# Value products of four key tiles in one block, and the order of the other products around them, in a gated cross-attention block with a mixture of experts

## The reference, cut to what matters

```
x: (32, 56, 128)   ctx: (32, 1500, 128)   16 heads of depth 8   160 experts, 8 chosen
q = layernorm(x) @ Wq.T + bq;  k = ctx @ Wk.T + bk;  v = ctx @ Wv.T + bv
scores = q.k / sqrt(8);  attn = softmax(scores);  out = (attn.v) @ Wo.T + bo
x = x + tanh(g_xattn) * out
logits = layernorm(x) @ router_w.T + expert_bias;  top 8 of sigmoid(logits), normalised, * 2.5
x = x + tanh(g_ffn) * (sum over experts of weight * silu(x @ w_gate.T) @ w_down.T + shared expert)
```

## Time and profile before

| what | value |
|---|---|
| median of 3 runs | 1172.58 us (1171.59 to 1176.96) |
| the profiled execution's own time | 1173.53 us |
| its span in the profile | 1172.0 us |
| instructions | 37843 |
| PE, DVE, ACT, POOL busy over the span | 91%, 83%, 72%, 51% |
| mean granted PE clock | 0.981 of full speed |

### The profile page before, as it was taken

One profiled execution on the slowest core, in us unless ns is written; L12 is line 12 of the kernel. 1 busy time (PEld: TensorE's weight loads), 2 busy tenths in 40 slices (PEclk: granted clock), 3 DMA queues, 4 the chain that ended last, 5 costly groups with the idle time before them and its releaser, 6 DMA issues.

```text
span 1172.0 us, 37843 instructions
## 1 busy us (share of the span) xinstructions
PE 1071.9 (91%) x12090; PEld 709.5 (61%) x12090; DVE 978.0 (83%) x1680; ACT 849.1 (72%) x1790; POOL 596.8 (51%) x1011
## 2 busy tenths in 40 slices
PE   1566989999999999999999999778999999999998
PEld 0244767777777777777777676544555555555554
DVE  2774878888888888888888789658999999999998
ACT  1334767776777777677777677557888888888887
POOL 7788588888889888888888871000000000000000
PEclk9988999999999999999999999889999999999999
DMA  8869778969889797897989852134767676767773
GB/s 130 144 118 182 156 131 177 163 151 160 157 174 166 154 163 149 169 171 151 159 158 174 150 118 61 19 124 131 235 231 234 223 240 221 238 228 232 231 226 125
DMA packets 200998, 197.04 MB, mean 168 GB/s; under 512 B 161183, under 2 KB 167391, under 8 KB 200966
## 3 DMA queue, kind: packets, MB, share of 16 engines
q1 hardware_dynamic: 189446, 175.64, 67.3%
q0 software_dynamic: 11520, 20.99, 6.4%
HBM read 109.96 MB, written 12.55 MB: 105 GB/s over the span
## 4 chain that ended last, share of the span: by engine, by line
PE 48%; issue 13%; POOL 13%; DVE 10%; SPq 10%; DMA 2%; ACT 1%; POOLq 1%; DVEq 0%; ACTq 0%
PE bank L1256 15%; PE bank L1228 15%; PE bank L1067 5%; PE bank L1081 5%; DVE part_max L835 5%; SPq L334 4%; PE bank L1098 4%; SPq L378 3%; DVE rec L936 2%; POOL q_st L574 2%; POOL ctx_parts L497 2%; PE bank L1134 2%; POOL w_in L458 2%; POOL w_in L460 2%; POOL q_blk L551 1%
## 5 line engine op out<-in xcount | busy, mean ns | idle before, releaser
L640 ACT ACTIVATE p_exp<-bank 125x448 f32<-125x448 f32 x768 | 400.4, 544 | 207.1 <-PE bank L1081 206.2
L835 DVE TENSOR_REDUCE part_max<-bank 128x1 f32<-128x500 f32 x672 | 419.8, 670 | 82.7 <-PE bank L1098 82.2
L1081 PE MATMUL bank<-q_st,k_stk 97*125 97x224 f16 x1536 | 277.3, 265 | 19.6 <-DMA q_st<-neg_row 9.9
L1098 PE MATMUL bank<-kparts,q_blk 128*128 128x500 f16 x672 | 256.8, 383 | 20.9 <-DVE part_max L835 17.4
L1081 PEld LDWEIGHTS bank<-q_st,k_stk 97*125 97x125 f16 x1536 | 198.4, 139 | 85.7 <-ACT p_exp L640 18.8
L1256 PE MATMUL bank<-ctT,w_ring 128*128 128x448 f16 x960 | 234.0, 353 | 3.0 <-DVE ctT L978 3.0
L729 ACT ACTIVATE ctT<-bank 128x448 f32<-128x448 f32 x320 | 174.0, 544 | 40.0 <-PE bank L1228 15.8
L978 DVE TENSOR_TENSOR ctT<-k_stk,ctT 128x448 f16<-128x448 f32 x320 | 197.6, 618 | 0.3 <-ACT ctT L735 0.2
L1067 PE MATMUL bank<-p_exp,v_sb 125*25 125x168 f32 (+1 forms) x6144 | 190.0, 265 | 0.6 <-ACT p_exp L640 0.6
L735 ACT ACTIVATE ctT<-k_stk 128x448 f16<-128x448 f32 x320 | 181.9, 568 | 3.5 <-DVE k_stk L972 3.4
L1228 PE MATMUL bank<-q_hi,w_ring 128*128 128x448 f16 x640 | 173.9, 354 | 2.4 <-ACT k_stk L717 2.4
(11 more groups left out here) (139 smaller groups left out, 1234.0 us busy)
## 6 DMA issues: line engine op xcount, KB each, us to landing
v_sb<-c_scratch SPq DMA_DIRECT2D x114, 448.0 KB, 4.0
k_stk<-kparts SPq DMA_DIRECT2D x384, 93.8 KB, 5.1
ctx_in<-in_ctx_dram SPq DMA_DIRECT2D x31, 750.0 KB
k_stk<-c_scratch SPq DMA_DIRECT2D x38, 448.0 KB, 3.9
w_scratch<-w_out POOLq DMA_DIRECT2D x80, 128.0 KB, 6.6
w_in<-in_L_ffn_w_gate_dram POOLq DMA_DIRECT2D x160, 32.0 KB, 3.9
w_in<-in_L_ffn_w_down_dram POOLq DMA_DIRECT2D x80, 64.0 KB, 7.0
v_sb<-c_scratch SPq DMA_DIRECT2D x6, 336.0 KB, 4.8
```

What stands on the lines that cost most here:

```text
L640: act.activation(p_exp[0:KP, j % PR, f * 448:(f + 1) * 448], ST[f][0:KP, 0:448], ACT.Exp).then_inc(exp_done, 1)
L835: v.reduce_max(part_max[:, i // NCH, i % NCH:i % NCH + 1], SM[i % NSM][:, 0:CK], axis=AX.X).then_inc(sm_maxed, 1)
L1081: last = pe.matmul(ST[f][0:KP, (g % 2) * GC:(g % 2 + 1) * GC], k_stk[0:97, u, g, j * KP:(j + 1) * KP], q_st[0:97, u, g, :, :].rearrange("p ...
L1098: pe.matmul(SM[i % NSM][:, 0:CK], rows, kparts[:, u, 0, c * CK:(c + 1) * CK], start=True, stop=True).then_inc(sm_done, 1)
```

## The change

- The ring `p_exp` gets six tiles instead of four; the raw weights, which are used at the start alone, lie in it instead of in a tensor of their own.
- AV products come in blocks of four key tiles, in slots 3, 7 and 11, instead of blocks of two, in slots 1, 3, 5, 7, 9 and 11.
- Key products move from slots 2, 6, 10 to 1, 5, 9; V products from 0, 4, 8 to 2, 6, 10.
- The spread and `normalise` move from slot 6 to 4, the spread ahead of the slot's second maximum; the output product moves from slot 11 to 8. The second V product of a step now waits for `normalise`, the third for the update of x.
- Maxima: `MAXIMA` gives their number in each slot, one in slots 5, 6 and 11, two in all others. The last one is now in slot 11, where PE also transposes the maximum.
- DVE's list follows: the copy and `normalise` stand ahead of the slot's second maximum; what empties the key bank comes after it.

```diff
-    PR = 4
+    PR = 6
+    AVB = 4
-    SPREAD_AT, OUT_AT, NEG_AT = 6, KT - 1, KT - 1
+    K_AT, V_AT = 1, 2
+    SPREAD_AT, OUT_AT, NEG_AT = 4, 8, KT - 1
+    MAXIMA = (2, 2, 2, 2, 2, 1, 1, 2, 2, 2, 2, 1)
...
-        w_raw = sb("w_raw", [128, 4, D])
...
-        q_tmp = e_words[:, NP * D:NP * D + TC]
+        q_tmp = e_words[:, (NP + 4) * D:(NP + 4) * D + TC]
+        w_raw = e_words[:, NP * D:(NP + 4) * D].rearrange("p (n c) -> p n c", c=D)
...
         def chunks_at(k, place):
-            i = 2 * k + place
-            return [i] if i < MT * NCH else []
+            return [sum(MAXIMA[:k]) + place] if place < MAXIMA[k] else []
...
# ACT
-                        if f == 0 and k % TPC == 1 and on(step, 1):
+                        if f == 0 and k % TPC == V_AT + 1 and on(step, 1):
                             values(back(step, 1), k // TPC)
...
-                    if k % TPC == 2:
+                    if k % TPC == K_AT:
                         act.wait_ge(kp_done, b * NCH + (c + 1))
...
# DVE
                     for i in chunks_at(k, 0) if on(step, 1) else []:
                         maxima(step, i)
-                    for i in chunks_at(k, 1) if on(step, 1) else []:
-                        maxima(step, i)
-                    evacuate(step, k - 1)
                     if on(step, 3) and k == LAG:
...
                     if on(step, 3) and k == SPREAD_AT:
                         normalise(step)
-                    if on(step, 1) and k == NEG_AT - 1:
+                    for i in chunks_at(k, 1) if on(step, 1) else []:
+                        maxima(step, i)
+                    evacuate(step, k - 1)
+                    if on(step, 1) and k == NEG_AT:
...
-                evacuate(step, KT - 1)
...
-                    if k % TPC == 2:
+                    if k % TPC == K_AT:
                         dve.wait_ge(k_hi_done, b * NCH + (c + 1))
...
# PE
-                    if values_there and jv % 2:
-                        value_product(bv_, jv - 1)
-                        value_product(bv_, jv)
+                    if values_there and jv % AVB == AVB - 1:
+                        for j in range(jv - AVB + 1, jv + 1):
+                            value_product(bv_, j)
+                    if on(step, 3) and k == SPREAD_AT:
...
+                            pe.wait_ge(v_copied, num(back(step, 1)) * NCH + 1)
...
+                        pe.wait_ge(o_copied, b + 1)
+                        pe.matmul(VB[:, 0:OC], den_spread[:, :], o_raw[:, :], start=True, stop=True).then_inc(spread_done, 1)
                     for i in chunks_at(k, 1) if on(step, 1) else []:
                         maxima(step, i)
...
-                    if on(step, 0) and k % TPC == 2:
+                    if on(step, 0) and k % TPC == K_AT:
...
-                    if on(step, 1) and k % TPC == 0:
+                    if on(step, 1) and k % TPC == V_AT:
                         until(pe, v_copied, b * NCH + c)
-                        if on(step, 4) and c == 0 and back(step, 4)[1] == 1:
-                            pe.wait_ge(x2_done, back(step, 4)[0] + 1)
-                        if on(step, 3) and c == 2:
+                        if on(step, 3) and c == 1:
                             pe.wait_ge(nrm_done, num(back(step, 3)) + 1)
+                        if on(step, 3) and c == 2 and back(step, 3)[1] == 1:
+                            pe.wait_ge(x2_done, back(step, 3)[0] + 1)
...
                     if on(step, 3) and k == OUT_AT and back(step, 3)[1] == 1:
...
-                            pe.wait_ge(v_copied, num(back(step, 1)) * NCH + NCH)
+                            pe.wait_ge(v_copied, num(back(step, 1)) * NCH + 2)
```

More of the change, by code:

```diff
@@ L1109, in body @@
                             maxima(step, i)
-                    if values_there and jv % 2:
-                        value_product(bv_, jv - 1)
-                        value_product(bv_, jv)
+                    if values_there and jv % AVB == AVB - 1:
+                        for j in range(jv - AVB + 1, jv + 1):
+                            value_product(bv_, j)
+                    if on(step, 3) and k == SPREAD_AT:
+                        b = num(back(step, 3))
+                        if on(step, 1):
+                            pe.wait_ge(v_copied, num(back(step, 1)) * NCH + 1)
+                        else:
+                            pe.wait_ge(v_copied, B * NCH)
+                            pe.wait_ge(x2_done, b // 2)
+                        pe.wait_ge(o_copied, b + 1)
+                        pe.matmul(VB[:, 0:OC], den_spread[:, :], o_raw[:, :], start=True, stop=True).then_inc(spread_done, 1)
                     for i in chunks_at(k, 1) if on(step, 1) else []:
@@ L1136, in body @@
                         last.then_inc(vp_done, 1)
-                    if on(step, 3) and k == SPREAD_AT:
-                        b = num(back(step, 3))
-                        if on(step, 1):
-                            pe.wait_ge(v_copied, num(back(step, 1)) * NCH + 2)
-                        else:
-                            pe.wait_ge(v_copied, B * NCH)
-                            pe.wait_ge(x2_done, b // 2)
-                        pe.wait_ge(o_copied, b + 1)
-                        pe.matmul(VB[:, 0:OC], den_spread[:, :], o_raw[:, :], start=True, stop=True).then_inc(spread_done, 1)
                     if on(step, 1) and k == NEG_AT:
```

## The result

| what | before | after |
|---|---|---|
| median of six runs each, on the same chip | 1173.40 us (1171.59 to 1176.96) | 1182.57 us (1179.32 to 1182.98) |
| the profiled execution's own time | 1173.53 us | 1179.32 us |
| its span | 1172.0 us | 1177.8 us |
| mean granted PE clock | 0.981 | 0.972 |

The ratio is 1.0082, 95% interval [1.0066, 1.0099]: slower by 9 us, and 1.6 us above the upper end of the range. The changed kernel once more on another chip gave 1178.05 us (1173.39 to 1182.00, six runs) against 1171.69, ratio 1.0049 [1.0033, 1.0066]. So the change costs 6 to 9 us, and the second median, 1178.05 us, lies inside the range.

The account below looks back on a forecast made before the run. PE and POOL were both taken as full with the same period, POOL's list deciding. The loop stayed unchanged and the tail gave -0.5: 1173.0 us profiled, median 1.0 lower, 1172.0 us; range 1167 to 1181.

Parts of the forecast that it names:

- POOL's list is untouched, a faster PE would wait for the row, and a slower one has room: Loop up to POOL's last one: no change, with POOL at 21.0 us a step against 20.7 of PE.
- AV blocks, -0.6 a step: PE's AV products: a block of four takes 1.68 us against 1.80, with fewer switches, saving 0.6 us a step.
- New waits, 1.4 us in place of 0.7: PE's list in the new order: waits in short slots, after key copies and for `normalise`, adding 0.7 us a step.
- DVE about 1 us idle before the copy, below the step: DVE's list: stands about 1 us until the block of four ends; 19 to 20 us a step, below the step.
- The ring of six, the output product, the transfers: nothing: `p_exp` with six tiles, output product moved to slot 8, SP's transfers: each claimed to cost or gain no time.
- Tail, -0.5: Last steps after POOL's last loop: a block of two no longer stands between scores in the very last, 0.5 us less.
- PE was the bound: Rival for the loop: POOL only looks full, its hidden waits shrink with PE; 17 us less, 1155 us; chance 0.10.
- V product of slot 6: Rival in PE's list: it waits for `normalise` 0.7 us instead of 0.4; each 0.5 beyond costs 14 us, 1186; chance 0.17.
- Switches not saved: Rival in the AV blocks: tiles wait for exponentials, PE's step is 21.3 us, total 1180 us; chance 0.03.
- The rule weighed: Skill page's rule for the most-contended engine: POOL leads at 87% against 74% weight loads of PE; no change in the sum.

Follow-up runs that it names:

- b_after: Changed kernel with the reciprocal written back into its own PSUM bank, so DVE's product has one SBUF operand: 1174.83 us, ratio 1.0025.
- bp_after: Changed kernel with POOL's store and loads of an expert preparation moved behind the next split, and the reciprocal in its PSUM bank: 1167.25 us, ratio 0.9959.
- the one edit tried: Changed kernel with AV blocks of two again in the last two steps alone: 1178.38 us, ratio 1.0064.
- bp_before: Kernel before with POOL's store and loads of an expert preparation moved behind the next split, and the reciprocal in its PSUM bank: 1161.22 us, ratio 0.9912.
- lighter list: Kernel before with POOL's store and loads of an expert preparation moved behind the next split or `q_st`: 1166.14 us, ratio 0.9949.
- the shorter wait: Changed kernel where the V product in slot 6 waits for the reciprocal instead of the product behind it: 1176.82 us, ratio 1.0042.

## Why the prediction was wrong, point by point

**The step that failed** is the one in the sum that reads "POOL's list is untouched, a faster PE would wait for the row, and a slower one has room". The list is untouched in its instructions, not in its time. POOL's two steps went from 41.31 to 41.69 us, because the change moved DVE's `o_nrm` from places where POOL computed nothing onto two of its casts. `b_after` shows it: with the product's second operand in its bank POOL is back at 41.36. With the collision POOL and PE are equally long again, the room for PE's longer order is gone, and what POOL loses in stoppages comes on top. The 24 steps can be parted into twelve steady pairs and the stoppages:

| us | steady pairs | stoppages | 24 steps |
|---|---|---|---|
| before | 12 x 41.34 = 496.1 | 5.9 | 502.0 |
| after | 12 x 41.66 = 499.9 | 5.1 | 505.0 |
| after, again | 499.9 | 4.4 | 504.3 |
| b_after | 12 x 41.68 = 500.2 | 2.4 | 502.6 |

With the collision taken away, what PE's longer period costs comes back through fewer stoppages all but 0.6 us: the room that the prediction counted on is there, and the loop costs close to the nothing that it forecast, instead of 2.3 to 3.0.

This step is not the whole miss. For the profiled execution I had 1173.0 us, and it took 1179.3. Of these 6.3 us the loop is 3.0, the tail 2.7 (2.2 more instead of 0.5 less), the start 0.6. In the second profile, 8.5 us above the one before, the loop is 2.3, the start 1.7, the three steps behind the loop 3.0 and the tail 1.5. And `b_after` is still 3 us slower than the kernel before (1.0025). Why the first six executions have a median 3.2 us above the profiled one no trace shows; with 1178.05 us, the other median, the range would have held.

**AV blocks, -0.6 a step.** Nearly right. A block of 64 matmuls takes 1.66 us to the next maximum (427.23 to 428.89 in the changed kernel), predicted 1.68; the scores ahead of it took 0.28 to 0.34, mostly 0.33, where I had 0.28, which takes about 0.1 us off the saving (an estimate from these rows).

**New waits, 1.4 us in place of 0.7.** Places right, sum nearly. The V product waits 0.35 (I had 0.4). PE's own steps are 20.53 and 21.15, predicted 20.4 and about 21.0: 41.68 for two instead of 41.4. `bp_after` gives the same 41.68 with POOL out of the way, so it is PE's order with DVE's and ACT's answers, and 0.28 us of it was missing from my walk. In 24 steps that is 3.4 us, nearly all that the order costs there; I had left it out of the sum because POOL's average of 42.3 would hide it.

**DVE about 1 us idle before the copy, below the step.** The idle time is right (1.15). That DVE does not matter is wrong. Its busy share says so and its place does not: a product of 0.57 instead of 0.39 makes PE's step longer by the same 0.18, in both orders, as long as PE waits for it.

**The ring of six, the output product, the transfers: nothing.** The ring alone changes nothing within 0.1%. The output product and the transfers were not tried alone.

**Tail, -0.5.** Wrong in sign: 1.5 and 2.2 us more in the two executions of the changed kernel, 0.5 and 1.4 more in the two with the bank. I read no granted clock there. PE is at half clock for 10.2 to 13.6 us there instead of 6.8, and blocks of four take 3.2 us in it instead of 1.7 (PE's timeline, after):

```profile
761.22 3.20 PE L1068 MATMUL bank<-p_exp,v_sb 125*25 125x168 f32 x64
```

That this makes the difference is argued from these rows; the one edit tried changed the clock as well as the blocks. The three steps before the last transpose scatter by 3 us from one execution to the next (69.4 and 72.3 for the same kernel), and remain open.

**The rivals.** *PE was the bound* (0.10): no. PE does have 41.35 of its own, as `bp_before` shows with POOL waiting for it, so its period was no image of POOL's, but with a shorter list for PE the new order is not shorter either. *V product of slot 6* (0.17): the sign is right and the wait has the size I gave it, 0.35 for 0.4. Its condition did not come true: PE's step, 20.83 on average, stayed under POOL's 21.0. The wait has a share all the same, 0.07 to 0.09 of the 0.16 us by which PE's step grew, and it is the way by which a longer product reaches PE. Without it the changed kernel still has 1.0042. *Switches not saved* (0.03): they are saved. That two full engines both get longer at once, by different causes, was in no case. Such a case, "both lists longer by 0.3 to 0.4 a pair", gives 12 x 0.35 = 4 us in the loop, 1176 us, and 1178 to 1179 with the tail as measured: nearer, and still short of 1182.57.

**The rule weighed** named POOL as the engine to relieve first. The lighter list alone gained 5.5 us, at the start, and nothing in the 24 steps; only with the collision removed did the loop give 5.8 us (502.0 to 496.2). Relieving the leader was right and not enough.

## What to carry to other kernels

When two engines are full with the same period, moving work of a third engine can lengthen either of them: look at what runs beside what, not only at who waits for whom. Before calling a list untouched, check that its instructions keep their neighbours on the other engines; here a product that read two operands from SBUF, moved by 2 us, cost POOL 0.36 us a pair of steps, and reading one of them from the bank took that away at no cost to the product. Take an edit as refuted only where no other list stands in its way: the shorter wait brought next to nothing beside a full POOL, and 14 us once POOL was free. An edit of the tail wants the granted clock read first: in these profiles PE's clock fell around pauses of 1.73 to 4.42 us, though not around each, and the edit meant for that stretch made the stretch longer.

A version that beats both kernels came out twice: 1161.22 us (the old order, lighter list, reciprocal in the bank) and 1161.37 us (the new order, lighter list, shorter wait), ratios 0.9912 [0.9887, 0.9936] and 0.9911 [0.9887, 0.9934].

## What the runs showed of the hardware that I had not expected

**DVE and POOL hold each other up when DVE's product has two operands in SBUF.** With one of them in PSUM it takes 0.390 to 0.393 us in all 96 cases of four kernels; with both in SBUF it takes 0.39 where POOL stands still. Beside POOL's work one of the two is longer, or both: mostly 0.56 to 0.68 for the product with the lighter list, or a product of 0.39 and a cast of 0.81 instead of 0.62, as at 411.57 in the changed kernel. The longest was beside `q_st` (DVE and POOL, the kernel before with the lighter list):

```profile
448.75 2.00 DVE L949 TENSOR_TENSOR o_nrm<-rec,o_raw 128x224 f32<-128x224 f32 x1
448.89 2.27 POOL L580 TENSOR_TENSOR q_st<-q_stk,stack_mask 96x224 f16<-96x224 f16 x4
```

Both are longer than alone, 0.39 and 2.10. The Trainium skill, page "SBUF — State Buffer", section "Who interferes with whom", says that a DVE instruction with two SBUF inputs meets a GpSimd instruction that reads SBUF, that one with at most one SBUF input outside the 2-port modes does not, and that the order of issue, not the kind of operation, decides who is blocked. On the first two the trace agrees, with the numbers above. On the third it is less plain: by the recorded starts the product was 0.14 us ahead, and it was the one that grew by 1.6 us, POOL's four instructions together by 0.17. This rule spoke against the change, or rather against its place on DVE's list, and I had not weighed it.

**An operand in PSUM costs that product nothing**: 0.391 us from the bank as from SBUF.

**The stretch at half clock in the tail has several lengths for one kernel**: 13.6 and 10.2 us in two executions of the changed kernel. By 5 us windows it was 6.8 or 6.9 in all five profiles of the old order with blocks of two, 10.3 in the one with blocks of four there, and 10.2 to 17.1 in the eleven of the new order. PE's pause ahead of it was longer before (4.42 us) than after (2.96), so its length alone does not set the stretch; what does stays open.
